# State scan: its results are stored from SyncE's queue at the end of each tile instead of from GpSimd's

## What is computed

```python
def step(state, inp):
    q_t, k_t, v_t, a_t, b_t = inp
    state = a_t[..., None, None] * state
    stored = jnp.einsum('bhij,bhj->bhi', state, k_t)
    delta = b_t[..., None] * (v_t - stored)
    state = state + jnp.einsum('bhi,bhj->bhij', delta, k_t)
    o_t = jnp.einsum('bhij,bhj->bhi', state, q_t)
    return (state, o_t)
...
_, outs = jax.lax.scan(step, state0, (qT, kT, vT, aT, bT))
```

## Time and profile before

| | |
|---|---|
| timed runs, median of 3 | 3787.32 us (3786.72 to 3790.21) |
| the profiled execution | 3794.78 us |
| its span, first to last instruction | 3793.0 us |
| PE busy (matmuls) | 2521.0 us, 66% |
| DVE busy | 2027.5 us, 53% |
| ACT busy | 1309.6 us, 35% |
| POOL busy | 791.6 us, 21% |
| mean granted TensorE clock | 0.745 |
| instructions | 108279 |

### The profile page before, as it was taken

The page is one execution under the profiler, slowest core; times in us unless marked ns, Lnnn a source line. Parts: engine busy times, 40 slices in busy tenths (PEclk is TensorE's granted clock), DMA queues, the critical chain, the costliest instruction groups (busy, mean ns, idle before and its releaser), DMA issues. The chain is left out here.

```text
span 3793.0 us, 108279 instructions
## 1 busy us (share of the span) xinstructions
PE 2521.0 (66%) x42132; PEld 1857.3 (49%) x42132; DVE 2027.5 (53%) x5459; ACT 1309.6 (35%) x3125; POOL 791.6 (21%) x1161
## 2 busy tenths in 40 slices
PE   5987883468888565755762887777760049999900
PEld 2554553445555354622441565555540049999800
DVE  2386887646666343464023677766763024444476
ACT  3766663346666433331000343333330012222200
POOL 0222221125555400000000110010103630000076
PEclk8998995555555577776765888888865579999955
DMA  3458888834444454524957211111114322222275
GB/s 105 162 183 257 263 277 275 275 101 102 100 100 103 104 161 146 174 99 164 414 232 285 97 59 58 58 58 58 58 46 145 105 79 69 72 69 71 64 224 162
DMA packets 387346, 534.51 MB, mean 141 GB/s; under 512 B 122140, under 2 KB 315640, under 8 KB 379384
## 3 DMA queue, kind: packets, MB, share of 16 engines
q1 hardware_dynamic: 308184, 343.88, 28.4%
q0 software_dynamic: 58688, 152.42, 12.8%
q10 hardware_dynamic: 20320, 36.44, 2.6%
HBM read 327.58 MB, written 216.15 MB: 143 GB/s over the span
## 5 line engine op out<-in xcount | busy, mean ns | idle before, releaser
L1108 ACT ACTIVATE ss_write_ps<-ss_state,ss_gammas 128x64 f32<-128x64 f32 x1024 | 263.3, 303 | 196.9 <-DVE ss_state L1156 196.9
L479 PE MATMUL dc_rows_ps<-dc_weights,dc_hT 128*128 128x512 f32 x512 | 264.0, 640 | 20.0 <-ACT dc_rows L608 17.4
L2728 PE MATMUL se_up_ps<-se_xT,se_w 128*128 128x128 f32 x2176 | 266.3, 276 | 0.1
L2736 PE MATMUL se_y_ps<-se_w,se_aT 128*128 128x256 f32 x1088 | 257.2, 379 | 0.0
L2728 PEld LDWEIGHTS se_up_ps<-se_xT,se_w 128*128 128x128 f32 x2176 | 254.8, 193 | 0.5 <-DVE se_w L2793 0.5
L2866 POOL DMA_INDIRECT cb_y<-scratch_ys,cb_to x128 | 137.3, 1073 | 564.1 <-DVE cb_to L2880 525.4
L2793 DVE COPY se_w<-mx_weights 128x2048 f32 x136 | 166.7, 1227 | 101.5 <-issue 101.5
L2736 PEld LDWEIGHTS se_y_ps<-se_w,se_aT 128*128 128x128 f32 x1088 | 196.4, 190 | 21.1
L1073 PE MATMUL ss_write_ps<-ss_solved,ss_k_rows 16*64 16x64 f32 x4096 | 180.7, 322 | 38.2 <-DVE ss_solved L1151 37.9
L1156 DVE TENSOR_TENSOR ss_state<-ss_write_ps,ss_block_mask 128x128 f32<-128x128 f32 x512 | 129.5, 291 | 135.7 <-PE ss_write_ps L1073 135.7
L2718 PE MATMUL se_xt_ps<-se_ident,se_xs 128*128 128x128 f32 x272 | 52.2, 275 | 223.0 <-DMA se_xs<-scratch_xs 223.0
(11 more groups left out here) (350 smaller groups left out, 5762.0 us busy)
## 6 DMA issues: line engine op xcount, KB each, us to landing
ex_w<-in_w_all SPq DMA_DIRECT2D x64, 1024.0 KB, 21.1
scratch_rows<-dc_rows POOLq DMA_DIRECT2D x64, 512.0 KB, 6.2
scratch_vw<-dc_out POOLq DMA_DIRECT2D x64, 512.0 KB, 6.7
dc_c_rows<-scratch_rows SPq DMA_DIRECT2D x64, 384.0 KB, 6.1
scratch_xs<-wa_zeros ACTq DMA_DIRECT2D x34, 512.0 KB, 14.6
se_xs<-scratch_xs SPq DMA_DIRECT2D x136, 128.0 KB, 2.0
scratch_ys<-se_y SPq DMA_DIRECT2D x136, 128.0 KB, 1.7
ss_wq_rows<-scratch_vw SPq DMA_DIRECT2D x128, 128.0 KB, 2.3
```

The source lines that it names most:

```text
L479: mm = pe.matmul(to, hT[i][:, k, :], weights[:, k, columns], start=(k == 0), stop=(k == HALVES - 1), skip_group_check=True)
L1108: ins = act.activation(write_ps[b][:, k, 0:WIDTH], state[b][:, k, :], ACT.Copy, scale=gammas[i][:, b, k, c:c + 1])
L2728: mm = pe.matmul(up_ps[i % 2][:, c * P:(c + 1) * P], w[i % (2 * AHEAD)][:, k * DFF + c * P:k * DFF + (c + 1) * P], xT[i % 2][:, k, :], sta ...
L2736: mm = pe.matmul(y_ps[i % 2][:, 0:DIM], aT[i % 2][:, c, :], w[i % (2 * AHEAD)][:, HALVES * DFF + c * DIM:HALVES * DFF + (c + 1) * DIM], st ...
```

## The change

The function `store` moves from the block of GpSimd to that of SyncE, and `tile_pair` of SyncE calls it last for every tile, behind the loads of the later tiles. GpSimd has no block in this stage any more. The wait for the last stores also goes to SyncE's end. `out_done` starts at 1 now like the others, and its waits are written with `at(...)`. Sizes, buffers and the number of DMAs stay.

```diff
--- before.py
+++ after.py
@@ -949,7 +949,7 @@
         consts, cleared = map(sem, ("consts", "cleared"))
         rows_in = [sem(f"rows_in{i}") for i in both]
         wq_in = [sem(f"wq_in{i}") for i in both]
-        out_done = [sem.from_zero(f"out_done{i}") for i in both]
+        out_done = [sem(f"out_done{i}") for i in both]
         turned, wq_low, wq_high, gammas_ready = map(sem, ("turned", "wq_low", "wq_high", "gammas_ready"))
         state_read = [sem(f"state_read{b}") for b in range(BATCH)]
         u_ready = [sem(f"u_ready{b}") for b in range(BATCH)]
@@ -997,6 +997,15 @@
                             sync.dma_start(u_rows[i][rows_of(u), b, :, :],
                                            vw_c[b, bass.ds(tile, 1), :, :, unit_column(u):unit_column(u) + WIDTH].rearrange("a t c f -> (a t) c f")).then_inc(rows_in[i], 16)
 
+                def store(tile, i):
+                    for b in range(BATCH):
+                        sync.wait_ge(u_ready[b], at((tile + 1) * N))
+                        for u in range(UNITS):
+                            for a in range(2):
+                                lines = slice(u * QUAD + a * CHUNK, u * QUAD + (a + 1) * CHUNK)
+                                to = solved_v[a][b, bass.ds(tile, 1), :, :, unit_column(u):unit_column(u) + WIDTH].rearrange("a t c f -> (a t) c f")
+                                sync.dma_start(to, solved[i][lines, b, :, :]).then_inc(out_done[i], 16)
+
                 def tile_pair(ii, left):
                     for i in both:
                         tile = ii * 2 + i
@@ -1007,6 +1016,7 @@
                             load_wq(tile + 3, 1 - i)
                         if left > 2 + i:
                             load(tile + 2, i)
+                        store(tile, i)
 
                 for i in both:
                     load_wq(i, i)
@@ -1017,23 +1027,8 @@
                     tile_pair(ii, 6)
                 tile_pair(PAIR - 2, 4)
                 tile_pair(PAIR - 1, 2)
-
-            @block.gpsimd
-            def _(pool):
-                def store(tile, i):
-                    for b in range(BATCH):
-                        pool.wait_ge(u_ready[b], at((tile + 1) * N))
-                        for u in range(UNITS):
-                            for a in range(2):
-                                lines = slice(u * QUAD + a * CHUNK, u * QUAD + (a + 1) * CHUNK)
-                                to = solved_v[a][b, bass.ds(tile, 1), :, :, unit_column(u):unit_column(u) + WIDTH].rearrange("a t c f -> (a t) c f")
-                                pool.dma_start(to, solved[i][lines, b, :, :]).then_inc(out_done[i], 16)
-
-                with pool.Fori(0, PAIR) as ii:
-                    for i in both:
-                        store(ii * 2 + i, i)
                 for i in both:
-                    pool.wait_ge(out_done[i], PAIR * STORES)
+                    sync.wait_ge(out_done[i], at(PAIR * STORES))
 
             @block.tensor
             def _(pe):
@@ -1144,7 +1139,7 @@
                         tile = ii * 2 + i
                         vec.wait_ge(rows_in[i], at((ii + 1) * LOADS))
                         if not (isinstance(ii, int) and ii == 0):
-                            vec.wait_ge(out_done[i], ii * STORES)
+                            vec.wait_ge(out_done[i], at(ii * STORES))
                         for c in range(N):
                             for b in range(BATCH):
                                 vec.wait_ge(state_read[b], at(tile * N + c + 1))
```

## The result

The changed kernel takes 3869.83 us in the median of five runs (3867.12 to 3873.06), against 3787.32 before (3786.36 to 3790.41): a ratio of 1.0214, 95% interval 1.0200 to 1.0228. It is 82.5 us slower, 0.8 us from the forecast of 3869.

The account below looks back on a forecast made before the run. The scan was taken as bound by a serial TensorE, VectorE, ScalarE ring at 15.44 us a tile, and after the change by SP's queue; 76 + 2.8 + 4 - 0.8 = +82 us on 3787.3 gave 3869 us, range 3848 to 3905.

Parts of the forecast that it names:

- The ring: Scan loop: serial chain TensorE, VectorE, ScalarE over 256 chunks, said to set the pace at 15.44 us a tile.
- Step 1: GpSimd's queue: 9.4 us of store issue a tile leaves it, hidden anyway, so VectorE gains nothing.
- Step 2: SP's queue: 16 stores cost 7.8 us a tile, besides 10.2 us of loads and 0.15 us of waits and jump.
- P: SP's service time for one tile in the scan loop, forecast at 18.15 us.
- Step 3: Scan loop: SP's queue, not VectorE's wait for stores to land, sets the pace, later by 1.6 us in two tiles.
- Loop and step 4: 28 tiles x (18.15 - 15.44) = +76 us, plus +2.8 us for code seen first in the loop's first pass.
- Step 5: Peeled tail, tiles 28 to 31: +2.5 to +5.1 us, taken as +4.
- Step 6: Stage's end: SP issues the last 16 stores sooner than GpSimd, -0.8 us.
- hidden after all: Rival: 36 DMAs fit on SP at 0.25 us or less a store; not slower, 3786.5 us; chance 5%.
- Cheap: Rival: a store on SP costs 0.37 us, 16.4 us a tile, some +31 us, 3818 us; chance 4%.
- dear stores: Rival: a store on SP costs GpSimd's 0.585 us, 19.7 us a tile, +127 us, 3914 us; chance 4%.
- Long DMAs in every pass: Rival: long DMAs recur in each loop pass on SP, 1.6 us more a tile, +45 us, 3914 us; chance 9%.

## Why the prediction was right, step by step

- *What bounds the kernel*: right. The ring kept its 15.4 to 15.5 us where SP's queue fitted into it (28 DMAs), and lost it where it did not (32, 34, 36), with stores as with loads.
- *Step 1, nothing gained on VectorE*: right, the 512 instructions that write `solved` take 221 ns in the median before and 222 after, and VectorE's busy time is 289.7 and 288.5 us in the stage.
- *Step 2, the stores*: 16 x 0.486 = 7.8 us, as forecast from SP's own loads with and without address work. Loads 10.30 us for 10.2. The waits and the loop's jump were mis-sized: from the last store to the next tile's first load it is 0.72 us (1016.58 to 1017.30) or 1.09, so beyond a usual step 0.42 us a tile in the mean, not 0.15. I had read them off GpSimd, where one issue takes longer; that they hide behind it there is a guess. P was 18.49, not 18.15.
- *Step 3, queue before data*: right. The stores landed and VectorE went on 1018.43 - 998.97 = 19.46 us after that tile's first service, so two tiles by the data chain are 19.46 + 14.96 = 34.4 us against 36.98 by the queue, 2.6 us later where 1.6 was forecast. Turning the order round confirmed it.
- *Loop and step 4*: (1331.39 - 811.12) / 28 = 18.58 us a tile, +88 us with the first pass in it (2.5 us of it, 2.8 forecast), for 76 + 2.8 = 79: +9.
- *Step 5, the tail*: from 1331.39 to the last state at 1380.8 (below) it is 49.4 us, +3.8 for +4.
- *Step 6, the end*: from the last state to the next stage 1392.3 - 1380.8 = 11.5 us against 1309.81 - 1291.6 = 18.2, so -6.7 and not -0.8. This step failed: I counted issues and took what follows the last one as fixed, while 5.28 us of it were GpSimd's drain, which goes with the stores. From the last store to the next stage it is 4.7 us (1387.60 to 1392.30) in place of 10.07, so 5.4 of the 6.7 us lie there; the other 1.3 are the issues, for which 0.8 was forecast.

```profile
1380.22 0.59 DVE L1151 TENSOR_TENSOR ss_state<-ss_write_ps,ss_block_mask 128x128 f32<-128x128 f32 x2 [0.39 <-PE ss_write_ps L1068]
...
1387.60 0.45 SPq L1007 DMA_DIRECT2D scratch_solved_q<-ss_solved  x1
1392.30 0.36 SPq L1248 DMA_DIRECT2D do_parity<-in_parity  x1
```

The stage's sum is 88 + 3.8 - 6.7 = +85.1, the forecast was +82. Two errors, +9 in the loop and -6 at the end, nearly cancel. The mechanism and the size of the loss were forecast, but that the time is hit to 0.8 us is luck: the parts miss by more, and the stage (+85.1), the profiled span (+75.0) and the medians (+82.5) differ among themselves by more than that. The range also has a slip: with all stores at 0.475 and no overhead P is 10.2 + 7.6 = 17.8 and not 17.6, so its lower end lies some 6 us too low; nothing measured is near it.

The rivals: *hidden after all* fell, since a store costs 0.486 us and not 0.25. The rule of the Trainium skill that it leaned on (DMA: Bandwidth & Descriptors, "Issuing engines are not separate DMA queues") holds that spreading issues over engines saves only sequencer time, which is usually small beside the DMA. The trace agrees for one DMA (0.49 us of issue, 1.8 us to landing) and not for the sum, since 16 of them were lost in every tile. *Cheap* and *dear stores* fell too, since 0.486 us lies between their 0.37 and 0.585. *Long DMAs in every pass* fell: behind the first pass the tiles keep a steady pace of 18.33 and 18.65 us, though SP never rests.

## What to carry to other kernels

Before moving DMAs to another queue, add up that queue's issues over one period of the loop that sets the pace (here 36 x about 0.5 us against 15.44 us), and compare with the period, not with the transfer or with the DMA engines' share, which was 0.42 and fell to 0.38. When such a queue is the bound, the wait names whichever transfer stands last in it; here reordering only renamed the wait, and fewer issues or a second queue helped. SP's issues are not counted as busy in the page, so its rest has to be read from its timeline.

## What the runs showed of the hardware that I had not expected

- GpSimd's DRAIN at the end of the stage took 5.28 us after 512 DMAs issued in it, 2.67 after 480 and also after 256, and 1.36 after 128. SP's took 7 ns in the same place in the kernel before, where it had only loads, and 13 ns in the changed one. The number of DMAs alone doesn't give the length, but what is left over after each 112 of them does: in every one of these traces GpSimd's issue pauses for 2.7 to 2.8 us after the 112th, 224th, 336th and 448th, as far as it gets (line below, of the kernel before; total, times, longest). Since the last such pause 64, 32, 32 and 16 DMAs had been issued, and 5.28, 2.67, 2.67 and 1.36 us are 0.08 us for each of them. No run varied this on purpose, and why it is so stays open.

```profile
POOL scratch_solved_q L1030 <- issue: 10.9, 4, 2.7
```

- An issue from SP costs about 0.5 us for 128 rows, of 256 bytes or of 1 KB, in either direction, and 0.75 for 256 rows of 1 KB. SP and ScalarE can issue at 0.48 us each at the same time.
- Stores of the same shape stand 0.41 and 0.57 us apart by turns on SP, although a unit's pair shares one address computation; the sum, not the single gap, was what the estimate hit.
